# Edge-feature rows of 128 columns, transposed by one DMA per window, and a running maximum kept in PSUM

## Chip, cores and metric

One NeuronCore of a Trainium2 chip runs the whole program. The metric is device time in microseconds (us), the median over runs. The document also uses one execution recorded by the hardware profiler: its page, its waits and its timelines.

## What is computed

A graph of 6,250 nodes and 206,250 directed edges, 16 features a node and an edge, goes through two layers. The second layer is the one that the change touches. Cut to what matters:

```python
h = relu(layernorm(x))                                  # (6250, 16)
w_m = (efeat @ W_msg  + b_msg ).reshape(E, 16, 16)      # per edge
w_a = (efeat @ W_attn + b_attn).reshape(E, 16, 16)
h_src = h[src][:, :, None]
e1, e2 = w_m * h_src, w_a * h_src
seg_max = segment_max(e2, dst)
ex = exp(e2 - seg_max[dst])
ft = segment_sum(e1 * ex / segment_sum(ex, dst)[dst], dst)
out = x + ft.sum(axis=1)
```

The first layer gathers a row of a precomputed table (node times relation weight) for every edge and sums the rows over each destination node.

## The kernel before, in words

**Windows.** Nodes are sorted by degree and laid on 128 partitions, so a partition holds one destination node. A *window* takes up to 48 edges (slots) of each of 128 nodes. A node with more edges goes through more windows, and a maximum and two sums are carried on. The number of slots that a window uses comes from a plan made on the chip. In the second layer they are counted in *halves* of 3 slots (`nh`, 6 to 16 of them) and *blocks* of 6 (`nb`). There are 50 windows; the loop over `pairs` has two of them in its body, `q` = 0 and 1.

**Edge features.** During the first layer, VectorE splits each edge's 16 features into bf16 parts (`split_chunk`), and SyncE writes them out as rows of `KE` = 100 bf16 columns into a DRAM tensor `ef6`, in 50 chunks. In the second layer GpSimd's queue fetches a window's rows by one indirect DMA into `efrow` (`edge_rows`): each partition receives 48 rows end to end. `edge_valid` on VectorE writes the last column of every row, which masks slots past the node's last edge.

**Transposes.** TensorE needs a slot's features along partitions. `transposes(w, t)` transposes eight slots with eight matmuls against an identity into PSUM (`psTb`), and ScalarE copies them to `efT` (`copy_T`), which has two buffers. Six such steps make a window. Those for window k+1 are issued inside window k: two after the weights of the message phase have begun, and one in each of the blocks 0 to 3 of the message phase. `efrow` has one buffer, so GpSimd waits for the last transposes before it fetches the next window's rows.

**Phase 1, scores.** For each half, TensorE makes the attention weights of 3 slots (`weights(0, q, h, ...)`, line 562, into one of two PSUM buffers `psW`), and in between adds the exponentials of the window before (`exp_sums`, line 568). VectorE multiplies the weights by the gathered node features (`times_h`, line 1187) into `score`. After each block it raises a running maximum `macc`, 6 slots wide in SBUF: line 1198 for blocks 0 and 1 together, line 1203 for each later block, line 1206 for an odd last half. Then it folds the 6 slots to one: 3 slots with 3 (helper line 787, 128x768), line 1210 and line 1211 (256 wide), and one more into `mnew` in PSUM (line 787 again), and line 1214 takes the difference to the old maximum.

**Phase 2, messages.** For each block VectorE subtracts the maximum (`from_max`, line 1218), multiplies the message weights by the node features (line 1187 again, into `prod`), and multiplies by the exponentials that ScalarE made (line 717; the product is line 1231). TensorE adds up the products (`prod_sums`, line 573) and closes each block with a small matmul that frees a `prod` buffer (line 620). At a window's end VectorE can go on only when TensorE has added the last products and has made the first weights of the next window.

**Gathers.** GpSimd's queue issues one indirect DMA per slot (line 359), one window ahead, paced by counters that VectorE raises.

Of the kernel before, what the change touches and what calls it, by code (L numbers as in the profile page):

```python
# [6 lines left out]
BF16 = mybir.dt.bfloat16  # L7
I32 = mybir.dt.int32
I16 = mybir.dt.int16
# [8 lines left out]
PN = 125  # L18
# [20 lines left out]
KE = 6 * D + 4  # L39
HI, MID, LO = 0, 3 * D, 5 * D  # L40
# [20 lines left out]
def build(nc, x, src, dst, efeat, etype, relw, loopw, relemb, wmsg, bmsg, wattn, battn, out, scratch):  # L61
    table_d, srcp_d, pairp_d, _, h2_d, first_d, info_d = scratch
    ef6_d = nc.dram_tensor("ef6", ((E + S) * KE,), BF16, kind="Internal").ap()
    ctx = ExitStack()
    with ctx:
# [27 lines left out]
        winhot, winrel = at(o + 2 * WCH, WCH, GC), at(o + 3 * WCH, WCH, GC)  # L93
        lhs = at(21200, 3 * GP, GC).rearrange("p (j n) -> p j n", j=3)
# [4 lines left out]
        ef6 = at(3 * CHR * D, CHR * KE).bitcast(BF16).rearrange("p (q r k) -> p q r k", q=2, k=KE)  # L99
# [7 lines left out]
        stage = sb("stage", [128, RING * BLK * IO + S * KE // 2 + S * GP])  # L107
        prod = stage[0:GP, 0:RING * BLK * IO]
        o2 = RING * BLK * IO
        efrow = stage[0:GP, o2:o2 + S * KE // 2].bitcast(BF16)  # L110
        efs = efrow.rearrange("p (s k) -> p s k", k=KE)
        o2 += S * KE // 2
        efT = stage[0:KE, o2:o2 + S * GP].bitcast(BF16).rearrange("k (q s n) -> k q s n", q=2, n=GP)
        tabgn = stage[127:128, o2:o2 + NW // 2].bitcast(I16)
# [13 lines left out]
        macc = work[0:GP, 0:BLK * IO].rearrange("p (s c) -> p s c", c=IO)  # L128

        def col256(j, n=1):  # L130
            return work[0:GP, BLK * IO + j * IO:BLK * IO + (j + n) * IO]
# [16 lines left out]
        tri = sb("tri", [PN, PN])  # L148
# [5 lines left out]
        nodei = sb("nodei", [PN, C + 1], I32)  # L154
        nodeid = sb("nodeid", [PN, C + 1])
        iotai = sb("iotai", [GP, NV], I32)
        iotaf = sb("iotaf", [GP, NV])
        firsts = sb("firsts", [PN, RPP])
        cnt = sb("cnt", [PN, C + 1])
        rowi = sb("rowi", [PN, C + 1], I32)  # L160
        start0 = sb("start0", [PN, C + 1])
        key = sb("key", [PN, C])
        rank = sb("rank", [PN, C])
        ranki = sb("ranki", [PN, C], I32)
# [28 lines left out]
        mnew = psT[0:GP, 8:10, :].rearrange("p a n -> p (a n)")  # L193
        psTb = psT[:, :, :].rearrange("p a n -> p (a n)").bitcast(BF16).rearrange("p (t s n) -> p t s n", t=3, n=128)
# [9 lines left out]
                 "hg0 hg1 hl0 hl1 h_free efT_ps efT_sb w_ready w_free d_ready c_ready "  # L204
# [30 lines left out]
        def _(sp):  # L235
# [19 lines left out]
            for a in range(2):  # L255
                sp.dma_start(ef6_d[E * KE + a * (S * KE // 2):E * KE + (a + 1) * (S * KE // 2)].rearrange("(a b) -> a b", a=1),
                             padrow[:, 0:S * KE // 4].bitcast(BF16)).then_inc(m["pad_out"], 16)
# [22 lines left out]
            ef6rows = ef6_d[0:E * KE].rearrange("(p c n) -> p c n", p=PN, c=ECH)  # L280
# [17 lines left out]
            for j in range(2):  # L298
                sp.wait_ge(m[f"ef6_out{j}"], 16 * (ECH // 2))

        @block.gpsimd
        def _(pool):
# [91 lines left out]
            def edge_rows(q):  # L395
                pool.indirect_dma_start(out=efrow, out_offset=None, in_=ef6_d.rearrange("(e k) -> e k", k=KE),
                                        in_offset=bass.IndirectOffsetOnAxis(ap=ebst[:, q:q + 1].bitcast(U32), axis=0)).then_inc(m["ef_in"], 16)
# [51 lines left out]
            with pool.Fori(0, pairs) as i:  # L449
                for q in range(2):  # L450
# [31 lines left out]
                    pool.wait_ge(m["efT_ps"], k * (S // 8) + (S // 8))  # L482
# [11 lines left out]
        def _(pe):  # L494
# [58 lines left out]
            def transposes(w, t):  # L553
                pe.wait_ge(m["efT_sb"], w * (S // 8) + (t + 1))
                for j in range(8):
                    last = nc.tensor.transpose(psTb[0:KE, t % 2, j, 0:GP], efs[:, 8 * t + j, :], identb[0:GP, 0:GP])  # L556
                last.then_inc(m["efT_ps"], 1)

            def weights(c0, q, h, at0):
                pe.wait_ge(m["w_free"], at0 + (h + 1))  # L560
                for j in range(HALF):
                    last = nc.tensor.matmul(psW[0:GP, h % 2, j * IO:(j + 1) * IO], efT[:, q, h * HALF + j, 0:GP],  # L562
                                            wst[:, c0:c0 + IO], start=True, stop=True)
# [14 lines left out]
            pe.wait_ge(m["valid_in"], 1)  # L578
            for t in range(S // 8):
                transposes(0, t)  # L580
            with pe.Fori(0, pairs) as i:
                for q in range(2):
# [4 lines left out]
                    pe.wait_ge(m["efT_sb"], k * (S // 8) + (S // 8 + 2))  # L587
# [13 lines left out]
                    pe.wait_ge(m["valid_in"], k + 2)  # L601
                    for t in range(2):
                        transposes(k + 1, t)
                    pe.wait_ge(m["sum_read"], k + 1)
                    nc.tensor.matmul(psS[0:GP, :], ident[0:GP, 0:GP], carry, start=True, stop=False)
                    for b in range(NBW):
# [6 lines left out]
                        if b + 2 < S // 8:  # L613
                            transposes(k + 1, b + 2)
# [17 lines left out]
        def _(act):  # L632
# [90 lines left out]
            for t in range(S // 8):  # L723
                copy_T(0, 0, t)
            act.wait_ge(m["m0_ready"], 1)
            with act.Fori(0, pairs) as i:
                for q in range(2):
# [14 lines left out]
                    for b in range(NBW):  # L742
# [7 lines left out]
                        if b < S // 8:  # L750
                            copy_T(k + 1, 1 - q, b)
# [533 lines left out]
```

## Time and profile before

| | |
|---|---|
| median of 3 runs | 5954.85 us (5950.09 to 5958.16) |
| the profiled execution | 5951.75 us, span 5949.9 us |
| mean granted TensorE clock | 0.935 |
| busy: TensorE matmul / VectorE / ScalarE / GpSimd | 46% / 58% / 23% / 70% |
| second layer, steady part | 3200 to 5900 us of the span |

Busy shares are averages over stages with different limits, so they are read stage by stage. In a timeline, "idle before" stands in brackets with what ended it. A start minus the start before it, on one engine, gives what an instruction costs in its place, and this is often less than its own duration, since neighbours overlap a little.

### The profile page before, as it was taken

To read this page: it belongs to the slowest core of one execution; us is meant where nothing else is said; L and a number is where in the kernel's file an instruction comes from. 1 tells how busy PE (TensorE), PEld (TensorE's weight loads), DVE (VectorE), ACT (ScalarE), POOL (GpSimd) and SP (SyncE) were. 2 spreads that over 40 slices of the span, in tenths; PEclk is the share of its full clock that TensorE was granted. 3 is DMA by queue.
4 is the path that set the end of the run, shared out by engine and by line. 5 is a ranking of instruction groups with operands and counts; after the bars stand their busy time and mean duration, and the time that the engine had idled before them with its cause. 6 is when DMAs were issued, how large, how long until landed. Compare 5 with 4: busy or idle time off the path is not lost.

```text
span 5949.9 us, 57446 instructions
## 1 busy us (share of the span) xinstructions
PE 2723.7 (46%) x13577; PEld 1930.7 (32%) x13578; DVE 3470.4 (58%) x4171; ACT 1369.4 (23%) x1709; POOL 4176.8 (70%) x3713
## 2 busy tenths in 40 slices
PE   2550000000000000000668888788888888878887
PEld 1110000000000000000446666565656565655565
DVE  8601222222222223332688888888888888888886
ACT  2540000000000000010223232333333333333333
POOL 2237777777777777765477878777777777777763
PEclk9999999999999999999978888888889888988998
DMA  4881111111111111110111111111111111111110
GB/s 145 285 264 27 29 22 28 29 30 35 29 29 36 29 36 36 36 34 19 21 22 22 22 24 28 22 22 30 22 22 30 22 30 22 30 22 30 30 30 19
DMA packets 157959, 251.69 MB, mean 42 GB/s; under 512 B 73726, under 2 KB 130563, under 8 KB 145156
## 3 DMA queue, kind: packets, MB, share of 16 engines
q0 software_dynamic: 126192, 100.10, 9.4%
q1 hardware_dynamic: 31711, 151.31, 7.7%
q8 instruction: 9, 0.15, 0.0%
q14 instruction: 15, 0.12, 0.0%
q10 hardware_dynamic: 32, 0.01, 0.0%
HBM read 113.57 MB, written 136.63 MB: 42 GB/s over the span
## 4 chain that ended last, share of the span: by engine, by line
POOL 28%; PE 23%; issue 15%; DVEq 14%; DVE 12%; DMA 5%; POOLq 1%; ACT 1%; SPq 0%; ACTq 0%
POOL gath L359 26%; PE psS L568 10%; PE psS L573 8%; DVEq L1228 7%; DVE stage L1187 4%; DMA table<-arena 4%; PE psW L562 3%; DVE stage L1231 3%; DVEq L1194 2%; DVEq L1187 1%; DVEq L1156 1%; PE psW L516 1%; DVEq L1143 1%; ACT arena L650 1%; DVE arena L1187 1%
## 5 line engine op out<-in xcount | busy, mean ns | idle before, releaser
L359 POOL DMA_INDIRECT gath<-h_dram,hidx x1695 | 2119.4, 1250 | 732.2 <-issue 556.0
L359 POOL DMA_INDIRECT gath<-table,blkidx x1646 | 1639.6, 996 | 508.2 <-issue 505.0
L556 PE MATMUL psT<-identb,stage 128*100 128x128 bf16 x2448 | 226.2, 251 | 2340.2 <-DVEq L1143 2321.9
L573 PE MATMUL psS<-stage,ident 128*128 128x256 f32 x3390 | 930.1, 430 | 169.6 <-DVE stage L1231 169.1
L556 PEld LDWEIGHTS psT<-identb,stage 128*100 128x100 bf16 x2448 | 201.6, 150 | 2380.7 <-DVEq L1143 2279.7
L568 PE MATMUL psS<-arena,ident 128*128 128x256 f32 x3390 | 823.8, 380 | 0.2 <-issue 0.2
L573 PEld LDWEIGHTS psS<-stage,ident 128*128 128x128 f32 x3390 | 705.3, 216 | 322.0 <-DVE stage L1231 212.4
L787 DVE TENSOR_TENSOR work<-gath 128x768 f32<-128x768 f32 x50 | 48.2, 965 | 1284.9 <-DMA gath<-table,blkidx 1284.9
L1187 DVE TENSOR_TENSOR arena<-psW,gath 128x768 f32 (+1 forms) x565 | 523.7, 952 | 438.0 <-PE psW L562 301.5
L562 PE MATMUL psW<-wst,stage 100*128 100x256 bf16 x3390 | 574.5, 290 | 241.6 <-DVE arena L1187 164.9
L717 ACT ACTIVATE arena<-arena 128x1536 f32<-128x1536 f32 (+1 forms) x294 | 421.4, 1433 | 894.4 <-DVE arena L1218 894.4
L568 PEld LDWEIGHTS psS<-arena,ident 128*128 128x128 f32 x3390 | 601.3, 190 | 69.1 <-issue 0.4
L1187 DVE TENSOR_TENSOR stage<-psW,gath 128x768 f32 (+1 forms) x565 | 514.1, 950 | 14.8 <-issue 14.8
L1231 DVE TENSOR_TENSOR stage<-stage,arena (+1 forms) x294 | 499.0, 1697 | 31.4 <-ACT arena L717 5.5
L1218 DVE TENSOR_TENSOR arena<-arena,psT 128x1536 f32 (+2 forms) x294 | 495.3, 1685 | 0.0
L678 ACT ACTIVATE work<-work 128x48 f32<-128x48 f32 x50 | 12.1, 243 | 2065.2 <-DVE work L1041 2065.2
L562 PEld LDWEIGHTS psW<-wst,stage 100*128 100x128 bf16 x3390 | 294.9, 101 | 519.7 <-DVE arena L1187 203.6
L1203 DVE TENSOR_TENSOR work<-work,arena 128x1536 f32<-128x1536 f32 x171 | 300.7, 1758 | 15.8
L712 ACT ACT_TABLE_LOAD x50 | 64.2, 1283 | 1042.1 <-PE psS L576 1042.1
L707 ACT COPY stage<-psT 100x1024 bf16<-100x1024 bf16 x306 | 301.2, 997 | 10.8 <-PE psT L556 10.8
L516 PE MATMUL psW<-stage,work 102*125 102x460 bf16 x400 | 182.4, 609 | 185.7 <-ACT arena L650 154.4
L650 ACT COPY arena<-psW 125x920 f32<-125x920 f32 x200 | 175.4, 927 | 203.8 <-DMA table<-arena 149.6
(227 smaller groups left out, 2395.4 us busy)
## 6 DMA issues: line engine op xcount, KB each, us to landing
table<-arena SPq DMA_DIRECT2D x50, 1610.0 KB
ef<-arena SPq DMA_DIRECT2D x50, 805.7 KB
gath<-h_dram,hidx POOLq DMA_INDIRECT x1695, 2.4
gath<-table,blkidx POOLq DMA_INDIRECT x1646, 2.4
arena<-in_edge_attr SPq DMA_DIRECT2D x50, 257.8 KB
table<-arena SPq DMA_DIRECT2D x50, 186.9 KB
arena<-first_dram POOLq DMA_DIRECT2D x1, 915.5 KB, 12.3
info<-info_dram POOLq DMA_DIRECT2D x2, 432.0 KB, 10.4
```

The source lines that it names most:

```text
L359: pool.indirect_dma_start(out=gath[:, q, s, :], out_offset=None, in_=rows, in_offset=bass.IndirectOffsetOnAxis(ap=idx[:, q, s:s + 1].bitca ...
L556: last = nc.tensor.transpose(psTb[0:KE, t % 2, j, 0:GP], efs[:, 8 * t + j, :], identb[0:GP, 0:GP])
L562: last = nc.tensor.matmul(psW[0:GP, h % 2, j * IO:(j + 1) * IO], efT[:, q, h * HALF + j, 0:GP], wst[:, c0:c0 + IO], start=True, stop=True)
L568: nc.tensor.matmul(psS[0:GP, 0:IO], ident[0:GP, 0:GP], score[:, q, s, :], start=False, stop=False)
L573: nc.tensor.matmul(psS[0:GP, IO:2 * IO], ident[0:GP, 0:GP], prod[:, c0:c0 + IO], start=False, stop=False)
L707: nc.scalar.copy(efT[:, q, 8 * t:8 * t + 8, 0:GP], psTb[0:KE, t % 2, :, 0:GP]).then_inc(m["efT_sb"], 1)
L717: nc.scalar.activation(v, v, ACT.Exp).then_inc(m["exp_done"], 1)
L1187: V.tensor_tensor(dst_ap.rearrange("p s (i o) -> p s i o", o=D), psW[0:GP, s, 0:HALF * IO].rearrange("p (s i o) -> p s i o", i=D, o=D), bc ...
L1203: V.tensor_tensor(macc, macc, score[:, q, ds(b * BLK, BLK), :], ALU.max).then_inc(m["scored"], 1)
L1218: V.tensor_tensor(blk, blk, mnew.unsqueeze(1).to_broadcast([GP, n, IO]), ALU.subtract).then_inc(m["sub_done"], 1)
L1228: V.drain()
L1231: V.tensor_tensor(pr, pr, score[:, q, ds(b * BLK, n), :].rearrange("p s c -> p (s c)"), ALU.mult).then_inc(m["q_ready"], 1)
```

## The change

- Rows of `ef6` have `KP` = 128 columns in place of 100. The 28 new columns are zero. DRAM tensor, chunk writes and the indirect fetch grow in that proportion.
- The 48 TensorE transposes and six ScalarE copies of a window go. SyncE issues one transposing DMA per window, from `efrow` (128 x 6144 bf16) to `efT[:, q]` (128 x 48 x 128). It waits for `valid_in` (the mask column is written) and `efT_free` (the weights of two windows ago have been read).
- TensorE waits at the head of a window for the whole transposed window (`efT_in`), and at its end has a 16-column matmul on zeros that raises `efT_free`. GpSimd waits for `efT_in` before it fetches the next rows.
- `macc` is 3 slots wide and lies in PSUM, in the banks that the transposes used. Each full block takes two 768-wide maxima with a drain between them, in place of one 1536-wide. Blocks 0 and 1 take three such instructions (one after block 0, two after block 1) in place of one of 1536. The final fold is three 256-wide maxima.
- Several small tiles of the first stages move into the arena, and ScalarE waits once for `idx_ready`.

```diff
-            def transposes(w, t):
-                pe.wait_ge(m["efT_sb"], w * (S // 8) + (t + 1))
-                for j in range(8):
-                    last = nc.tensor.transpose(psTb[0:KE, t % 2, j, 0:GP], efs[:, 8 * t + j, :], identb[0:GP, 0:GP])
-                last.then_inc(m["efT_ps"], 1)
-            def copy_T(w, q, t):
-                act.wait_ge(m["efT_ps"], w * (S // 8) + (t + 1))
-                nc.scalar.copy(efT[:, q, 8 * t:8 * t + 8, 0:GP], psTb[0:KE, t % 2, :, 0:GP]).then_inc(m["efT_sb"], 1)
...
+            def transpose_rows(w, q):
+                sp.wait_ge(m["valid_in"], w + 1)
+                sp.sem_inc(m["passed"], 1)
+                sp.wait_ge(m["efT_free"], w + 1)
+                sp.sem_inc(m["passed"], 1)
+                sp.dma_start_transpose(efT[:, q, :, :], efrow).then_inc(m["efT_in"], 16)
...
-                    pool.wait_ge(m["efT_ps"], k * (S // 8) + (S // 8))
+                    pool.wait_ge(m["efT_in"], k * 16 + 16)
                     pool.sem_inc(m["passed"], 1)
                     edge_rows(1 - q)
...
-                    pe.wait_ge(m["efT_sb"], k * (S // 8) + (S // 8 + 2))
+                    pe.wait_ge(m["efT_in"], k * 16 + 16)
...
+                    nc.tensor.matmul(psS[0:GP, IO:IO + D], zero[:, 0:GP], zero[:, 0:D], start=False, stop=False).then_inc(m["efT_free"], 1)
...
-            V.memset(ef6[:, :, :, KE - 1:KE], 0.0)
+            V.memset(ef6[:, :, :, KE - 1:KP], 0.0)
...
+                    def raise_max(b, halves=2):
+                        for s in range(halves):
+                            if s:
+                                V.drain()
+                            last_op = V.tensor_tensor(macc, macc, score[:, q, ds(b * BLK + HALF * s, HALF), :], ALU.max)
+                        return last_op
+
                     scores(0)
+                    V.tensor_tensor(macc, score[:, q, 0:HALF, :], score[:, q, HALF:BLK, :], ALU.max)
                     scores(1)
-                    V.tensor_tensor(macc, score[:, q, 0:BLK, :], score[:, q, BLK:2 * BLK, :], ALU.max).then_inc(m["scored"], 2)
+                    raise_max(1).then_inc(m["scored"], 2)
...
-                        V.tensor_tensor(macc, macc, score[:, q, ds(b * BLK, BLK), :], ALU.max).then_inc(m["scored"], 1)
+                        raise_max(b).then_inc(m["scored"], 1)
...
                     edge_valid(k + 1, 1 - q)
-                    tt(macc[:, 0:HALF, :], macc[:, 0:HALF, :], macc[:, HALF:BLK, :], ALU.max)
+                    V.drain()
                     dve.wait_ge(m["mold_ready"], k + 1)
-                    V.tensor_tensor(macc[:, 0, :], macc[:, 0, :], macc[:, 1, :], ALU.max)
-                    V.tensor_tensor(macc[:, 2, :], macc[:, 2, :], mold, ALU.max)
-                    V.drain()
-                    tt(mnew, macc[:, 0, :], macc[:, 2, :], ALU.max)
+                    tt(ratio, macc[:, 2, :], mold, ALU.max)
+                    tt(ratio, macc[:, 1, :], ratio, ALU.max)
+                    tt(mnew, macc[:, 0, :], ratio, ALU.max)
```

## Rows read from the trace of the kernel before

**Rows 1.** The page, busy time, share of the span and instructions of each engine.
```profile
PE 2723.7 (46%) x13577; PEld 1930.7 (32%) x13578; DVE 3470.4 (58%) x4171; ACT 1369.4 (23%) x1709; POOL 4176.8 (70%) x3713
```

**Rows 2.** Busy time by stretch: first layer, steady second layer; clock, DMA, GB/s last.
```profile
370.00:2708.00 2338.00, 43.12 (x92) 14.70 (x91) 615.84 (x1398) 192.29 (x253) 1690.84 (x1700) 1.00 0.16 39
...
3200.00:5900.00 2700.00, 2212.05 (x11500) 1632.76 (x11500) 2313.28 (x2265) 898.45 (x1130) 2024.88 (x1600) 0.88 0.12 26
```

**Rows 3.** Waits of VectorE, 3200 to 5900 us: total us, times, longest.
```profile
DVE arena L1187 <- PE psW L562: 273.8, 180, 5.3
```

**Rows 4.** Timeline of VectorE in phase 1 of one window: start, us, instruction.
```profile
4546.23 0.96 DVE L1187 TENSOR_TENSOR arena<-psW,gath 128x768 f32<-128x768 f32 x1 [0.67 <-PE psW L562]
...
4552.49 1.76 DVE L1203 TENSOR_TENSOR work<-work,arena 128x1536 f32<-128x1536 f32 x1
4554.17 1.81 DVE L1187 TENSOR_TENSOR arena<-psW,gath 128x768 f32 x2
```

**Rows 5.** Timeline of VectorE, the fold at the end of that phase 1.
```profile
4563.70 0.96 DVE L787 TENSOR_TENSOR work<-work 128x768 f32<-128x768 f32 x1
4564.73 0.43 DVE L1210 TENSOR_TENSOR work<-work 128x256 f32<-128x256 f32 x1
...
4565.56 0.43 DVE L787 TENSOR_TENSOR psT<-work 128x256 f32<-128x256 f32 x1
...
4566.41 1.75 DVE L1218 TENSOR_TENSOR arena<-arena,psT 128x1536 f32<-128x1536 f32 x1
```

**Rows 6.** The page, costliest groups: count, then busy us, mean ns, idle before.
```profile
L556 PE MATMUL psT<-identb,stage 128*100 128x128 bf16 x2448 | 226.2, 251 | 2340.2 <-DVEq L1143 2321.9
...
L1203 DVE TENSOR_TENSOR work<-work,arena 128x1536 f32<-128x1536 f32 x171 | 300.7, 1758 | 15.8
```

**Rows 7.** Groups of VectorE by line over the whole span.
```profile
L1198 DVE TENSOR_TENSOR work<-arena 128x1536 f32<-128x1536 f32 x50 | 88.0, 1760 | 4.6
...
L1206 DVE TENSOR_TENSOR work<-work,arena 128x768 f32<-128x768 f32 x23 | 22.0, 958 | 2.1
```

**Rows 8.** Timeline of TensorE where one window ends and the next begins.
```profile
4541.67 0.28 PE L620 MATMUL psS<-zero 1*128 1x256 bf16 x1
4542.45 0.50 PE L562 MATMUL psW<-wst,stage 100*128 100x256 bf16 x3 [0.50 <-issue]
```

**Rows 9.** Timeline of VectorE, the first product of two other windows.
```profile
4288.23 0.96 DVE L1187 TENSOR_TENSOR arena<-psW,gath 128x768 f32<-128x768 f32 x1 [3.59 <-PE psW L562]
...
4418.89 0.96 DVE L1187 TENSOR_TENSOR arena<-psW,gath 128x768 f32<-128x768 f32 x1 [5.28 <-PE psW L562]
```

**Rows 10.** TensorE by stretch: busy us (count), granted clock, DMA share, GB/s.
```profile
4406.00:4413.00 7.00, 4.14 (x21) 1.00 0.07 5
4413.50:4417.00 3.50, 3.34 (x8) 0.53 0.10 4
```

**Rows 11.** All engines by stretch while edge rows come in; DMA share, GB/s last.
```profile
4544.00:4546.00 2.00, 2.00 (x14) 1.61 (x12) 0.96 (x1) 0.00 (x0) 1.64 (x2) 1.00 1.00 274
4546.00:4548.00 2.00, 2.00 (x13) 1.70 (x12) 1.10 (x2) 0.00 (x0) 1.45 (x2) 1.00 0.85 349
```

**Rows 12.** DMA queues (packets, MB, share of 16 engines) and issues (median us to landing).
```profile
q0 software_dynamic: 126192, 100.10, 9.4%
...
stage<-ef,ebst POOLq DMA_INDIRECT x51, 6.0
```

**Rows 13.** Timelines of VectorE and TensorE in one of the shortest windows.
```profile
5795.14 0.33 DVE L1142 TENSOR_SCALAR stage<-iotaf,erem 128x48 bf16<-128x48 f32 x1
...
5827.29 0.50 PE L562 MATMUL psW<-wst,stage 100*128 100x256 bf16 x3
```

**Rows 14.** Timelines of GpSimd and VectorE early in the second layer.
```profile
2921.37 0.94 POOL L359 DMA_INDIRECT gath<-h_dram,hidx  x1 [9.40 <-DVE work L1198]
2922.61 2.37 POOL L359 DMA_INDIRECT gath<-h_dram,hidx  x1 [0.30 <-issue]
...
2986.88 1.82 DVE L1187 TENSOR_TENSOR arena<-psW,gath 128x768 f32 x2 [14.57 <-DMA gath<-h_dram,hidx]
```

More of the change, by code:

```diff
@@ L39 @@
 KE = 6 * D + 4
+KP = 128
 HI, MID, LO = 0, 3 * D, 5 * D
@@ L93, in build @@
         winhot, winrel = at(o + 2 * WCH, WCH, GC), at(o + 3 * WCH, WCH, GC)
+        tri = at(21600, PN, PN)
+        nodei = at(21725, C + 1, PN, I32)
+        nodeid = at(21776, C + 1, PN)
+        iotai = at(21827, NV, GP, I32)
+        cnt = at(21955, C + 1, PN)
+        rowi = at(22006, C + 1, PN, I32)
+        start0 = at(22057, C + 1, PN)
+        key = at(22108, C, PN)
+        rank = at(22158, C, PN)
+        ranki = at(22208, C, PN, I32)
         lhs = at(21200, 3 * GP, GC).rearrange("p (j n) -> p j n", j=3)
@@ L105, in gtmp @@
             return at(o + NROW + (C + 1) * ROW + i * C * D, GC * D, GP).rearrange("p (c d) -> p c d", d=D)
-        stage = sb("stage", [128, RING * BLK * IO + S * KE // 2 + S * GP])
+        stage = sb("stage", [128, RING * BLK * IO + S * KP // 2 + S * GP])
         prod = stage[0:GP, 0:RING * BLK * IO]
         o2 = RING * BLK * IO
[L110 to L114, printed above, removed]
+        efrow = stage[0:GP, o2:o2 + S * KP // 2].bitcast(BF16)
+        efs = efrow.rearrange("p (s k) -> p s k", k=KP)
+        o2 += S * KP // 2
+        efT = stage[0:KP, o2:o2 + S * GP].bitcast(BF16).rearrange("k (q s n) -> k q s n", q=2, n=GP)
         tabtmp = stage[0:1, 4608:4608 + NW // 2].bitcast(I16)
@@ L299, in _ @@
                 sp.wait_ge(m[f"ef6_out{j}"], 16 * (ECH // 2))
+            def transpose_rows(w, q):
[4 more added lines that the diff above has]
+                sp.dma_start_transpose(efT[:, q, :, :], efrow).then_inc(m["efT_in"], 16)
+            sp.wait_ge(m["win_ready"], 16)
+            pairs = sp.value_load(npair[0:1, 0:1], min_val=(GC + 1) // 2, max_val=NW // 2 - 2)
+            with sp.Fori(0, pairs) as i:
+                for q in range(2):
+                    transpose_rows(2 * i + q, q)
+            transpose_rows(2 * pairs, 0)
+            sp.wait_ge(m["efT_in"], pairs * 32 + 16)
+            sp.sem_inc(m["passed"], 1)
         @block.gpsimd
@@ L561, in weights @@
                 for j in range(HALF):
-                    last = nc.tensor.matmul(psW[0:GP, h % 2, j * IO:(j + 1) * IO], efT[:, q, h * HALF + j, 0:GP],
+                    last = nc.tensor.matmul(psW[0:GP, h % 2, j * IO:(j + 1) * IO], efT[0:KE, q, h * HALF + j, 0:GP],
                                             wst[:, c0:c0 + IO], start=True, stop=True)
@@ L722, in _ @@
             act.reg_mov(cumb, 0)
-            for t in range(S // 8):
-                copy_T(0, 0, t)
             act.wait_ge(m["m0_ready"], 1)
+            act.wait_ge(m["idx_ready"], 2)
             with act.Fori(0, pairs) as i:
@@ L761, in _ @@
             V = nc.vector
-            for name, n in (("tbl_sb", 2), ("l0_math", 2), ("h_free", 2), ("efT_sb", 2), ("w_free", 2), ("q_free", RING)):
+            for name, n in (("tbl_sb", 2), ("l0_math", 2), ("h_free", 2), ("efT_free", 2), ("w_free", 2), ("q_free", RING)):
                 dve.sem_inc(m[name], n)
```

41 lines of the change are left out of this document (11 added, 30 removed).

## The prediction

> **What bounds the kernel now.** I read the page's busy shares first [rows 1]. GpSimd leads with 70% over the span, which is no answer, since the stages differ. So I read the busy times by stretch next [rows 2]. In the first layer (370 to 2708 us) GpSimd's queue is busy 1691 of 2338 us, issuing gathers one after the other, and everything else waits for them. In the second layer, 3200 to 5900 us, VectorE is busy 2313 of 2700 us and TensorE 2212. The change is worked out there. VectorE's waits then say when it isn't VectorE that counts [rows 3]: 273.8 us of waiting for the weights, in 180 places over 45 windows, so four in each. A window's timeline shows which four. One is the handover between windows, 3 to 5 us. The other three are 0.67 us each, in the second to fourth half of phase 1 [rows 4], where TensorE gives a half every 0.67 + 0.96 = 1.63 us and VectorE needs 0.96. From the fifth half on, VectorE waits for TensorE no more until the window ends. So a window's length is VectorE's instruction stream, plus the handover, plus three short waits.
>
> **The change part by part.** All sums are made against the profiled execution, 5951.75 us, 3 us under the median of the runs.
>
> *Transposes and copies.* 2448 TensorE transposes, 226 us of busy time [rows 6], and ScalarE's six copies a window go. I cost this at nothing. They lie in phase 2 and just before it, where VectorE has no gap and TensorE waits for VectorE's products; ScalarE is busy 898 of 2700 us [rows 2]. The cover is VectorE's stream. Without it a window would gain up to 226/51 = 4.4 us. No transpose stands in the handover or between the first halves, the places where VectorE waits.
>
> *Running maximum.* A full block's maximum now costs 4554.17 - 4552.49 = 1.68 us from start to start [rows 4]. The new one is a 768-wide instruction with a drain behind it, then another. With SBUF operands the first costs 4564.73 - 4563.70 = 1.03 [rows 5], and a second that the next instruction overlaps costs about 0.87 (0.96 less the 0.08 by which 1.76 exceeds 1.68). Together 1.90, or 0.22 more; I take 0.23, since writing to PSUM in place of SBUF adds at most 0.01 to a 256-wide one, 0.43 each [rows 5]. No row reads and writes PSUM in one VectorE instruction. Reading it costs nothing visible: 0.96 from PSUM [rows 4], 0.958 from SBUF [rows 7]. Bounds for the pair are 1.86 and two full 1.03, so 0.18 to 0.38 more. It applies to 171 later blocks [rows 6] and to block 1 in 50 windows [rows 7], all behind the last short wait: 221 x 0.23 = +51 us (40 to 84). The maximum after block 0 takes about 1.0 us and falls between the second and third half, where 0.67 is waiting. The third half starts some 0.35 late, and the fourth waits for TensorE anyway, so 0 (up to 17 for 50 windows). The 23 odd halves stay at one 768-wide instruction, 0.
>
> The Trainium skill, "VectorE: DVE Perf Modes", section on the TRN2 errata, gives a VectorE instruction a fixed part of 58 cycles with an SBUF source and 120 with a PSUM source at 0.96 GHz. By it each PSUM-source instruction is an estimated 0.065 us dearer, and some 615 of them (442 in pairs, 23 odd, 150 in folds) would add 40 us, for a total near 6007. The rows do not agree, with 0.96 against 0.958 us at the same width, and the sum goes by them.
>
> *Fold.* Before, from the 768-wide fold to the subtraction, 4566.41 - 4563.70 = 2.71 us [rows 5]. After: a drain on an empty pipe (about 0.05), three dependent 256-wide maxima at 0.51 each (0.43 plus 0.08 of drain) and the difference at 0.34, together 1.92. Saved 0.79, times 50 is -40 us (-36 to -43).
>
> *Handover.* TensorE gets one small matmul between the last products and the next weights. Its wide sister takes 0.28 us and is followed by 0.50 us in which the engine waits for its own instructions [rows 8]. Below 0 nothing is possible, above 0.28; I take 0.1, so +5 us (0 to 14).
>
> *The transposing DMA.* It moves 128 x 6144 x 2 B = 1.57 MB. No row shows one. The nearest from below is the row fetch, which runs at about 311 GB/s [rows 11] (its 1.23 MB land 6.0 us after issue [rows 12]), giving 5.0 us plus about 2 for issue and landing: 7. From above: every 256 B piece as a packet of its own, at the gathers' mean of 9.4% x 16 x 5949.9 / 126192 = 71 ns of an engine [rows 12], so 6144 x 71 ns / 16 = 27 us. I take 15, nearer the fetch than the gathers. Its cover is phase 2. In one of the shortest windows (47.5 us long), mask written at 5795.5, first weights at 5827.3: 31.8 us [rows 13]. The mean window is 2700/45 = 60 us, with some 40 in the same proportion. So 0 at either bound. If it were late, TensorE stands at the head of the window, and behind it the weights for VectorE. GpSimd's new wait stands behind a whole window of gathers. Behind it are the row fetch, the output scatter and the next gathers, and it is the looser of the two. SyncE has nothing else queued.
>
> *Wider rows.* A chunk write grows by 28%, under 1 us at 311 GB/s; it lies beside GpSimd's stream, 0. The row fetch goes from 6.0 to about 7.5 us and has the 15 us and more of phase 1, 0. The larger memset happens once, 0 to 2 us. ScalarE's wait for `idx_ready` is over before it has work.
>
> *GpSimd relieved.* A gather takes 2.37 us, not 0.94, where it meets the 1536-wide maximum with its two SBUF inputs [rows 14]. That ends for the maxima. It counts only where VectorE waits for gathers, which after the first window is 14.57 us [rows 14] and once more a few. -4 us (-18 to 0).
>
> Sum: +51 - 40 + 5 - 4 = +12. 5951.75 + 12 = 5964; against the median 5955 + 12 = 5967. I give 5966. What a measurement of this kernel can tell from no change is about 0.2%, 12 us, so this lies at its edge.
>
> **The rivals.**
>
> *TensorE's clock at the handover (the faster side).* VectorE waits 5.28 us there in some windows and 3.59 in others that end alike [rows 9], two of 48. In the former the clock fell to half after a thinly used stretch (4.14 of 7 us busy at full clock, then 0.53) [rows 10]. About 20 of 48 windows have the fall. Which ones depends on how gaps fall together, and window lengths change. If all lost it, 14 even ones x 1.65 and 9 others at about 0.8 give -31: 5966 - 31 = 5935. Against it: the last two blocks never had many transposes, and their gaps stay. It decides once eight or more windows lose the fall and GpSimd's relief gives its 18. The reverse, all windows falling, is +30: 5996. Stretches with weights and no transposes ran at full clock [rows 10], so I see no fall in mid-phase.
>
> *PSUM maxima at their dear bound.* 84 in place of 51, the third half's 17 and the handover's 14: 5966 + 33 + 17 + 9 = 6025. For it: nobody shows a PSUM-to-PSUM instruction. Against it: each side alone costs nothing.
>
> *The transposing DMA outlasts phase 2.* The engines may cut the write into pieces smaller than 256 B, since a transposed row is scattered over partitions; this is also the case in which the change does not do what it says. From 31.8 us on, short windows lengthen. At 50 us, against some 40 of cover on average, it is 10 x 49 = +490: 6450. If pieces were 64 B, four times 27 is 108, and then (108 - 40) x 49 = +3330: 9300. For it: nothing here bounds the pieces. Against it: the row fetch ran at 274 to 349 GB/s.
>
> **How the numbers follow.** The sum as it stands has 0.62, with a range of its own from 5943 to 6000. Clock and relief together 0.13, dear maxima or a worse clock 0.12, late DMA 0.13. The predicted time is the first's. The range 5938 to 6025 leaves out the late DMA and a little of the fast side, 0.18 in all. Faster by over 0.2% (under 5943): 0.04 of the first and 0.12 of the second, 0.16. Within: 0.38 of the first and 0.02 of others, 0.40. Slower: 0.20 + 0.12 + 0.12, 0.44.
>
> **What would show it.** Pairs of 768-wide maxima at 1.90 us from start to start; a fold of 1.9 us; no wait of TensorE for `efT` at a window's head, and the DMA landing within 27 us; handover waits still spread from about 3 to 5.3 us; phase 2 without new waits. The prediction is wrong if VectorE has gaps before its first product that end with the transposing DMA, or if a PSUM maximum takes more than 1.03 us, or if the handover waits move together to one side.

## The result, and the profile after

The changed kernel takes 5975.89 us (median of 8 runs, 5972.98 to 5982.7), the kernel before 5955.94 us in the same comparison: ratio 1.0035, 95% interval 1.0024 to 1.0046, so 14 to 27 us slower. The forecast was 5966 us, with a range of 5938 to 6025. On the third of the four chips that the experiments used, one execution of the kernel before took 7991 us, the ten others 6266 to 6302; it enters no ratio. The profiled execution has a span of 5974.9 us and a mean granted clock of 0.925.

The page's busy times, against [rows 1], and the busy times by stretch, against [rows 2]:

```profile
PE 2587.0 (43%) x11179; PEld 1765.6 (30%) x11180; DVE 3512.5 (59%) x4392; ACT 1092.2 (18%) x1403; POOL 3938.9 (66%) x3713
```
```profile
370.00:2708.00 2338.00, 48.53 (x103) 16.46 (x103) 604.87 (x1375) 196.44 (x251) 1697.64 (x1703) 1.00 0.18 45
3200.00:5900.00 2700.00, 2093.34 (x9395) 1489.32 (x9394) 2341.33 (x2442) 658.13 (x862) 1824.22 (x1608) 0.86 0.26 57
```

In the steady stretch TensorE is relieved of 119 us and ScalarE of 240. Neither shows in the time, for VectorE sets the pace there, and its busy time rises by 28. VectorE in phase 1 of one window, against [rows 4], and in its fold, against [rows 5]:

```profile
4502.26 0.96 DVE L1184 TENSOR_TENSOR arena<-psW,gath 128x768 f32<-128x768 f32 x1 [3.60 <-PE psW L573]
4503.89 0.96 DVE L1184 TENSOR_TENSOR arena<-psW,gath 128x768 f32<-128x768 f32 x1 [0.67 <-PE psW L573]
4504.94 0.97 DVE L1201 TENSOR_TENSOR psT<-arena 128x768 f32<-128x768 f32 x1
4505.82 0.95 DVE L1184 TENSOR_TENSOR arena<-psW,gath 128x768 f32<-128x768 f32 x1
4507.14 0.96 DVE L1184 TENSOR_TENSOR arena<-psW,gath 128x768 f32<-128x768 f32 x1 [0.38 <-PE psW L573]
...
4512.01 2.01 DVE L1197 TENSOR_TENSOR psT<-psT,arena 128x768 f32<-128x768 f32 x2
4513.93 1.81 DVE L1184 TENSOR_TENSOR arena<-psW,gath 128x768 f32 x2
...
4523.54 0.34 DVE L1139 TENSOR_SCALAR stage<-iotaf,erem 128x48 bf16<-128x48 f32 x1
4524.05 0.93 DVE L784 TENSOR_TENSOR work<-psT,work 128x256 f32<-128x256 f32 x2 [0.17 <-issue]
4525.05 0.43 DVE L784 TENSOR_TENSOR psT<-psT,work 128x256 f32<-128x256 f32 x1
...
4525.89 1.75 DVE L1222 TENSOR_TENSOR arena<-arena,psT 128x1536 f32<-128x1536 f32 x1
```

Read starts, not durations. A pair of maxima takes 4513.93 - 4512.01 = 1.92 us where one instruction took 1.68: 0.24 more, 221 times, +53 us. The maximum after block 0 (line 1201) fills what was a wait for TensorE, and of the three short waits one and a half are left: the fourth half starts 4507.14 - 4502.26 = 4.88 us after the first, just as before (4547.86 - 4542.98). From the mask (line 1139) to the subtraction (line 1222) it is 4525.89 - 4523.54 = 2.35 us. Before, the mask started here:

```profile
4563.25 0.33 DVE L1142 TENSOR_SCALAR stage<-iotaf,erem 128x48 bf16<-128x48 f32 x1
```

To the subtraction at 4566.41 that is 3.16 us, so 0.81 less now, 50 times, -40 us.

The groups of VectorE by line: all 465 in-place PSUM maxima (2 x 221 and 23 odd halves), mean 967 ns, against 958 from SBUF [rows 7].

```profile
L1197 DVE TENSOR_TENSOR psT<-psT,arena 128x768 f32<-128x768 f32 x465 | 449.5, 967 | 38.9
```

The handover on TensorE, against [rows 8], and the waits of VectorE, 3200 to 5900 us, against [rows 3]:

```profile
4501.50 0.28 PE L623 MATMUL psS<-zero 1*128 1x256 bf16 x1
4501.62 0.17 PE L625 MATMUL psS<-zero 1*128 1x16 bf16 x1
4501.72 0.50 PE L573 MATMUL psW<-wst,stage 100*128 100x256 bf16 x3
```
```profile
DVE arena L1184 <- PE psW L573: 225.3, 133, 5.3
```

Three waits a window are left of four, and VectorE's waits for gathers or the transposing DMA do not appear in the stretch at all. That DMA on SyncE's queue, the DMA share by stretch around it (share and GB/s last), and the queues, against [rows 12]:

```profile
4524.08 7.33 SPq L307 DMA_TRANSPOSE stage<-stage  x1
```
```profile
4524.00:4526.00 2.00, 0.00 (x0) 0.00 (x0) 1.73 (x5) 1.69 (x2) 0.00 (x0) 0.90 0.39 76
4526.00:4528.00 2.00, 0.00 (x0) 0.00 (x0) 2.00 (x3) 0.74 (x2) 0.94 (x1) 0.50 1.16 217
4528.00:4530.00 2.00, 1.34 (x2) 0.50 (x2) 1.46 (x4) 1.16 (x1) 1.69 (x2) 0.50 1.14 210
4530.00:4532.00 2.00, 0.73 (x1) 0.00 (x0) 1.27 (x3) 0.00 (x0) 1.39 (x3) 0.50 1.15 210
4532.00:4534.00 2.00, 1.64 (x6) 0.56 (x6) 1.90 (x2) 0.00 (x0) 1.63 (x2) 0.50 0.61 96
```
```profile
q1 hardware_dynamic: 346687, 243.09, 15.3%
q0 software_dynamic: 126192, 117.65, 10.0%
```

The window's rows are transposed between some 4525 and 4533 us; TensorE wants them 30 us later. Queue q1 had 31,711 packets before, so the 51 transposing DMAs are 6,176 packets each. At 1.57 MB that is 255 B a packet on average, which would fit 6,144 pieces of 256 B and 32 small ones; no row shows the split.

**The window as a whole.** The timelines between 3200 us and the last handover of the stretch hold 44 whole windows in each kernel. Mean us of one, and VectorE's idle time in it by place (from the waits in brackets, summed; the finish is the short arithmetic that closes the window before):

| kernel | window | handover | phase 1 | fold and finish | phase 2 | rest: VectorE's stream |
|---|---|---|---|---|---|---|
| before | 60.58 | 4.09 | 2.01 | 0.71 | 0.41 | 53.37 |
| after | 60.81 | 3.99 | 1.05 | 0.91 | 0.41 | 54.45 |

That is +0.23 us a window, +10 for the 44. From the first handover to the last, with the early windows that wait for gathers, the two profiles differ by less: 2970.5 against 2962.7 us, +7.8. Behind the last handover the changed kernel takes 75.9 us against 74.3, +1.6. The other 15.6 us of the 25 between these two executions stand before the first handover (2928.47 against 2912.90), 11.2 of them in the stage in which the window tables and the relation table are built.

### The profile page after: what moved, and what is told of

It reads as the page before. It is cut to its first block, busy times and chain, and to the rows that moved or that the text cites. A ratio compares the mean times of both kernels' runs of the same rounds, so it can differ in the third digit from the quotient of the medians.

```text
span 5974.9 us, 52495 instructions
## 1 busy us (share of the span) xinstructions
PE 2587.0 (43%) x11179; PEld 1765.6 (30%) x11180; DVE 3512.5 (59%) x4392; ACT 1092.2 (18%) x1403; POOL 3938.9 (66%) x3713
## 4 chain that ended last, share of the span: by engine, by line
POOL 28%; PE 20%; issue 15%; DVEq 15%; DVE 13%; DMA 5%; POOLq 1%; ACT 1%; SPq 0%; ACTq 0%
POOL gath L376 26%; PE psS L584 8%; PE psS L579 8%; DVEq L1232 6%; DMA table<-arena 4%; DVE stage L1184 4%; DVEq L1191 3%; PE psW L573 3%; DVE stage L1235 3%; DVE psT L1197 2%; DVEq L1184 1%; DVEq L1143 1%; PE psW L533 1%; ACT arena L654 1%; DVE work L784 1%
## 5 line engine op out<-in xcount | busy, mean ns | idle before, releaser
L376 POOL DMA_INDIRECT gath<-h_dram,hidx x1695 | 1915.9, 1130 | 992.8 <-issue 549.3
L584 PE MATMUL psS<-stage,ident 128*128 128x256 f32 x3390 | 982.4, 449 | 256.3 <-DVE stage L1235 255.9
L584 PEld LDWEIGHTS psS<-stage,ident 128*128 128x128 f32 x3390 | 739.9, 226 | 448.0 <-DVE stage L1235 324.8
L1197 DVE TENSOR_TENSOR psT<-psT,arena 128x768 f32<-128x768 f32 x465 | 449.5, 967 | 38.9
L610 PE MATMUL psS<-efraw,ident 128*128 128x512 f32 x100 | 103.6, 1140 | 277.6 <-DVEq L1153 277.6
L533 PEld LDWEIGHTS psW<-stage,work 102*125 (+1 forms) x400 | 59.6, 206 | 317.2 <-ACT arena L654 242.1
L347 POOL DMA_INDIRECT info_dram<-arena x50 | 59.0, 1180 | 118.3 <-DVEq L910 94.1
```

Source lines behind the costliest of these rows:

```text
L376: pool.indirect_dma_start(out=gath[:, q, s, :], out_offset=None, in_=rows, in_offset=bass.IndirectOffsetOnAxis(ap=idx[:, q, s:s + 1].bitca ...
L533: last = nc.tensor.matmul(psW[0:PN, u % 2, 512 * a:512 * a + PIECE], hT6[:, ds(2 * t + j, 1), 0:PN].rearrange("k a n -> k (a n)"), relW6[: ...
L584: nc.tensor.matmul(psS[0:GP, IO:2 * IO], ident[0:GP, 0:GP], prod[:, c0:c0 + IO], start=False, stop=False)
L1197: last_op = V.tensor_tensor(macc, macc, score[:, q, ds(b * BLK + HALF * s, HALF), :], ALU.max)
```

## The experiments

The first four were timed on one chip, the next four on another, with the kernel before beside each. Ratios are to that kernel.

**1. The kernel before, again** (a comment changed).

> The kernel before, once more, for a second profile of it. In the first pair of profiles the changed kernel is 25 us longer, and 11.2 us of that stand before its first layer begins (first product of the first layer at 526.7 in place of 515.5 us) and 15.6 us before the second handover of the second layer (2928.5 in place of 2912.9). Theory A, the extra in the table stage is chance of single executions: this profile puts the first product anywhere from 510 to 530 us. Theory B, it belongs to the changed kernel: this profile puts it within 2 us of 515.5.

Measured: 5964.77 us, ratio 1.0000 (0.9990 to 1.0011). The last copy of the table stage, at 436.27 us in the profile of before and 447.51 in that of after, came here at 459.15, and the first handover at 2937.22. The first product of the first layer stands at 538.4 us, later than either theory had it. A later beginning of this size comes without the change. In the four profiles with the early stages of before (number 8 is one) the first handover stands at 2912.90, 2920.20, 2923.27 and 2937.22 us, in five of the changed kernel and its variants at 2921.04 to 2928.47, so no shift there stands out from that scatter. The 44 windows have 60.64 us.

**2. Placement alone**, **3. wide rows alone**, **4. the changed kernel with the maximum as before.** Number 2 is the kernel before with the larger DRAM tensor, number 3 the kernel before with 128 columns and the moved tiles, TensorE still transposing. Number 4 keeps the transposing DMA; it holds a table of window codes of 3,072 entries in place of 4,608, and this input uses some 50. Number 4 also brings back the 1536-wide maxima that read two SBUF inputs.

```diff
# 2
-    ef6_d = nc.dram_tensor("ef6", ((E + S) * KE,), BF16, kind="Internal").ap()
+    ef6_d = nc.dram_tensor("ef6", ((E + S) * 128,), BF16, kind="Internal").ap()[0:(E + S) * KE]
# 3
+KP = 128
-    ... KE (ef6_d, ef6, efrow, efs, ef6rows, edge_rows)
+    ... KP
# 4, against the changed kernel
-        macc = psT[0:GP, 0:2 * HALF, :]...
+        macc = work[0:GP, 6 * IO:6 * IO + BLK * IO]...
-                    raise_max(1).then_inc(m["scored"], 2)
+                    V.tensor_tensor(macc, score[:, q, 0:BLK, :], score[:, q, BLK:2 * BLK, :], ALU.max).then_inc(m["scored"], 2)
...
```

> The kernel before with only the DRAM tensor ef6 made as large as the changed kernel's, 128 columns a row; its rows stay at 100 columns and end to end, the rest is never touched. No instruction differs. Theory A (chance) and theory C (the wider rows' own traffic in the first layer): no change, ratio 1.000 within 0.001. Theory B (the place of tensors in DRAM sets the rate of the table writes): first product of the first layer at about 526 us and 8 to 12 us longer.

> One part of the change alone: rows of 128 columns in DRAM, in the chunk writes, in the fetch and in efrow, and the small tiles moved into the arena. The 48 TensorE transposes, the six copies and the running maximum in SBUF stay. If my sum holds (wider rows cost nothing) and the table stage is chance: 0 to +2 us. If the wider rows or their place cost what the profiles show ahead of the second layer: +8 to +15 us, with the first layer's end 4 us and the table's end up to 11 us later.

> The changed kernel with the running maximum undone: six slots wide in SBUF, one 1536-wide maximum a block and the old fold. The transposing DMA stays. For room the table of window codes is cut from 4608 to 3072 entries, of which this input uses some 50. The sum says that the new maximum costs 221 x 0.24 = +53 us and its fold saves 50 x 0.81 = 40 us, so undoing both takes 13 us off the changed kernel: ratio to the kernel before about 1.0013, near 5963 us. Rival: the extra lies in the transposing DMA or in the stages before it; then this stays at 5972 to 5976 us. Under the clock rival the handover waits would differ as a group, by 15 us or more.

Measured: 5961.91 us, 0.9996 (0.9987 to 1.0006); 5959.96 us, 0.9997 (0.9988 to 1.0006); 5968.97 us, 1.0007 (0.9997 to 1.0016). By these intervals neither place nor width costs more than 4 us, the row fetch of 28% more bytes included. With the maximum back in SBUF, 0.0007 is left, of 0.0035 in the first comparison and 0.0028 in number 5. So the maximum and its fold are the main part, 13 to 17 us of 17 to 20, where the two terms make 13. Number 4 and the changed kernel were not timed on the same chip, so this is a difference of two ratios. The transposing DMA with all that it took away is worth 0.0007, its interval reaching to nothing.

Number 4 also tells what relieves GpSimd. Its steady stretch, all engines, GpSimd's queue the fifth:

```profile
3200.00:5900.00 2700.00, 2092.61 (x9411) 1499.82 (x9410) 2308.07 (x2252) 656.92 (x861) 2023.43 (x1606) 0.85 0.26 57
```

The queue is busy 2023 us, as before the change (2025), against 1824 with the maximum in PSUM. It is the new maximum that gives GpSimd 200 us back, and not the transposing DMA.

**5. The changed kernel, again.**

> The changed kernel, measured again beside the one before. If the first comparison (ratio 1.0035) tells what the change costs, this one gives 1.002 to 1.005. If it came from chance beginnings of the window-table stage (11 us later in the profiled execution of the changed kernel, and up to 12 us later in another execution of the kernel before itself), it gives under 1.002, and the profile's steady part, from the second handover between windows to the last, still shows about 8 us more than the 2962 to 2965 us of the kernel before.

Measured: 5978.57 us, 1.0028 (1.0018 to 1.0038). The first theory holds. The same 44 windows in all profiles of this kind, mean us of one:

| kernel | window | handover | window without handover and phase 2's idle time |
|---|---|---|---|
| before | 60.58 | 4.09 | 56.08 |
| 1, before again | 60.64 | 4.14 | 56.09 |
| 2, placement alone | 60.64 | 4.14 | 56.09 |
| 3, wide rows alone | 60.80 | 4.28 | 56.11 |
| 4, changed, maximum as before | 60.76 | 4.22 | 56.13 |
| changed | 60.81 | 3.99 | 56.41 |
| 5, changed again | 60.90 | 4.08 | 56.41 |
| 7, changed, four small matmuls | 60.84 | 4.06 | 56.38 |

The last column repeats to some hundredths and moves with the maximum alone: 0.28 us between number 4 and the changed kernel, 14 us for 50 windows. The handover scatters by up to 0.2 us between profiles of kernels with equal medians (numbers 2 and 3 against each other: 0.14; before against 3: 0.19), 9 us for 48 handovers, so the sum of one profile does not settle 10 us.

**6. Four transposing DMAs in a row per window.**

```diff
-                sp.dma_start_transpose(efT[:, q, :, :], efrow).then_inc(m["efT_in"], 16)
+                for n in range(4):
+                    sp.dma_start_transpose(efT[:, q, :, :], efrow).then_inc(m["efT_in"], 16)
+                    if n < 3:
+                        sp.wait_ge(m["efT_in"], w * 64 + 16 * (n + 1))
```

> The changed kernel with the transposing DMA of each window given four times, each after the one before has landed. One pass is read off the DMA engines' busy stretch as 9 to 10 us, so four take 37 to 40 us, against a cover of 31.8 us in the shortest window and of some 40 us in most. Theory that the single pass is wholly hidden with 22 us or more to spare: 5 to 30 us slower than the changed kernel, all of it in waits of TensorE at its first weights of a window, and nothing on VectorE's waits for the gathers. Rival that the pass already costs something by itself, because it takes DMA engines and the SBUF from the gathers: three more passes cost three times that at the gathers too, VectorE's waits for gathered rows grow from 132 us, and the kernel is 40 us or more slower.

Measured: 6127.38 us, 1.0287 (1.0271 to 1.0303), 149 us more than number 5. Its stretches of 1 us (DMA share and GB/s last) show one pass from edge to edge, and the start of the next:

```profile
4524.00:4525.00 1.00, 0.00 (x0) 0.00 (x0) 0.85 (x3) 0.99 (x2) 0.00 (x0) 0.79 0.04 7
4525.00:4526.00 1.00, 0.00 (x0) 0.00 (x0) 0.93 (x3) 0.69 (x2) 0.00 (x0) 0.50 1.12 215
...
4532.00:4533.00 1.00, 0.96 (x6) 0.34 (x4) 0.90 (x2) 0.00 (x0) 0.69 (x2) 0.50 0.68 125
4533.00:4534.00 1.00, 0.40 (x2) 0.00 (x0) 1.00 (x1) 0.00 (x0) 0.60 (x1) 0.50 0.08 8
...
4535.00:4536.00 1.00, 1.00 (x4) 0.73 (x4) 1.00 (x1) 0.00 (x0) 0.77 (x1) 0.50 0.90 175
```

A pass keeps the DMA engines busy 7.7 us, the next starts 10.1 us after its start, and the fourth ends at 4562.6, 39 us after the mask. TensorE's waits in the stretch 3200 to 5900 us:

```profile
PE psW L577 <- DMA stage<-stage: 85.3, 24, 8.2
```

So at some 40 us the third rival's mechanism is there: a window takes 64.12 us, VectorE's handover wait 6.58 and its phase 1 wait 1.75, and its stream is unchanged (54.48). The gathers were not held up: VectorE's waits for them are 124.2 us (132.2 with one pass). The size was far above what I expected (5 to 30), since I had set the cover at 40 us for most windows, and it is about what four passes take, so about every second window pays. A late window also costs more than TensorE's wait: behind one of 3.18 us, from 5628 to 5631 us, the granted clock was 0.58, and VectorE's second wait there was 1.94 us in place of 0.67.

**7. Four small matmuls at the handover in place of one.**

```diff
+                    for _ in range(3):
+                        nc.tensor.matmul(psS[0:GP, IO:IO + D], zero[:, 0:GP], zero[:, 0:D], start=False, stop=False)
```

> The changed kernel with four of the small 1-row, 16-column matmuls at the end of each window in place of one. In the trace the one takes 0.17 us and moves the next matmul by 0.10 us. Theory that it stands on the path (VectorE waits there for the first products' weights): three more cost 3 x 0.10 x 50 = 15 us, ratio 1.0025 to the changed kernel. Rival that they overlap, or that the handover's length is set by the granted clock alone: within 5 us of the changed kernel.

Measured: 5972.44 us, 1.0026 (1.0015 to 1.0037), so not slower than number 5; my own theory fell. The distance from the closing matmul of the last block to the next weights, the most frequent value of 44 or 45 handovers, is 0.21 us before, 0.22 after and 0.29 here. A small matmul takes 0.01 to 0.03 us there, for it begins before its neighbour has ended. The mean distance, with the handovers in which TensorE stands still on its own, is 0.54 us before, 0.57 to 0.59 in two profiles of the changed kernel and 0.60 here.

**8. Early weights, on the kernel before.** The first two groups of weights of the next window are made ahead of the last block's product sums, so that VectorE finds them.

```diff
-                        with pe.If(nb > b):
+                        with pe.If(nb > b + 1):
                             pe.wait_ge(m["q_ready"], tb + (b + 1))
...
+                    for h in range(2):
+                        weights(0, 1 - q, h, tn * 4)
+                    pe.wait_ge(m["q_ready"], tn)
+                    for b in range(MINB - 1, NBW):
+                        with pe.If(nb > b):
+                            with pe.If(nb < b + 2):
+                                prod_sums(2 * b)
...
```

> The kernel before, with the next window's first two groups of four weight products made ahead of the last block's product sums, so that VectorE finds them at the handover. My reading of the handover is that VectorE stands still there for 3.6 us on average (183 us over the 45 handovers listed past 3200 us, 1 us of it for the end of its own pipe) while TensorE finishes the product sums and then makes the weights. Theory: nearly all of that goes, 45 to 50 times 3 us = 130 to 170 us, 5790 to 5830 us. Rival: the two groups need psum space and the granted clock that the last product sums need as well, or the finish of the window then waits for sum_done, and VectorE loses at the maximum or at the finish what it gains at the handover: 0 to 60 us gained.

Measured: 5981.34 us, 1.0047 (1.0033 to 1.0061). Both theories had expected a gain. The handover's wait fell from 4.1 to 1.31 us a window, and phase 1's rose from 2.01 to 4.84. TensorE and VectorE there:

```profile
4851.92 0.28 PE L576 MATMUL psS<-zero 1*128 1x256 bf16 x1
4855.51 0.50 PE L562 MATMUL psW<-wst,stage 100*128 100x256 bf16 x3 [3.31 <-issue]
```
```profile
4850.40 1.82 DVE L1206 TENSOR_TENSOR arena<-psW,gath 128x768 f32<-128x768 f32 x2 [2.32 <-PE psW L562]
4856.05 0.96 DVE L1206 TENSOR_TENSOR arena<-psW,gath 128x768 f32<-128x768 f32 x1 [3.83 <-PE psW L562]
```

Behind the last product sums TensorE stands 3.31 us and waits for no other engine. The granted clock was 1.00 before and during this stretch, 0.64 in the 2.5 us behind it and 0.73 in the 3 us after that, so the weights that follow are late twice over. My edit finds the last block by a row of nested tests there; in the kernel before, the tests for the last blocks come while TensorE waits for VectorE. That the tests make the gap is my reading; number 10 moves them and has no gap.

**9. Two transposing DMAs**, as number 6. **10. Early weights with the test inside the loop over blocks**, where TensorE has time. **11. The same on the changed kernel. 12. Number 10 again.**

```diff
                         with pe.If(nb > b):
+                            if b + 1 >= MINB:
+                                with pe.If(nb < b + 2):
+                                    for h in range(2):
+                                        weights(0, 1 - q, h, tn * 4)
                             pe.wait_ge(m["q_ready"], tb + (b + 1))
```

> The changed kernel with the transposing DMA of each window given twice. In the run with four passes one pass keeps the DMA engines busy 7.7 us at some 207 GB/s, the next begins 10.1 us after it, and four end 40.1 us after the mask of the last column; TensorE waited for them in about half of the windows. Two end after about 20 us, the next window's first weights are due after 31.8 us in the shortest window. Theory that a pass costs nothing until it lands too late: within 6 us of the changed kernel, ratio to the kernel before 1.002 to 1.004, and no wait of TensorE for the DMA. Rival that the traffic itself costs time, by holding up gathers or SBUF accesses of VectorE: a third of what three more passes cost (149 us), so some 50 us more, ratio 1.011.

> The kernel before, with the next window's first two groups of weight products made ahead of the last block's product sums, now tested for inside the loop over blocks, so that the tests run while TensorE waits for VectorE anyway. In the first form TensorE stood 3.3 us in its own sequencer behind the last product sums (in the window looked at) and VectorE lost there, at the third half, what it gained at the first. Theory that those tests were all that ate the gain: the third half comes 2 us or more earlier in each window, 80 to 130 us gained, 5830 to 5880 us. Rival that the sequencer's time belongs to the start of a window and is only no longer hidden: the wait before the third half stays near 3 us and the time within 20 us of the kernel before.

> The same edit on the changed kernel. The weights of the next window now need the transposing DMA 4 to 6 us earlier, against 22 us to spare in the shortest window, so that costs nothing. Theory: it gains as much here as on the kernel before, and the difference of the two stays 10 to 20 us. Rival: the maximum's cost of 0.24 us per block pair or the fold's gain changes its worth where the handover no longer sets VectorE's start, and the two come out equal within 6 us.

> The kernel before with early weights and the test inside the loop over blocks, measured again, because the last comparison came from a chip on which the kernel before itself took 6283 us and VectorE had long waits that no semaphore explains, in every stage. In the window read there TensorE goes from the last product sums to the third group of weights with no gap, and VectorE waits 2.38 + 1.18 + about 0.67 us over the first four halves where the kernel before waits 4.08 + 3 x 0.67 = 6.09 us on average. On a chip on which the kernel before takes 5950 to 5970 us the theory gives 2 to 3 us per window, 100 to 150 us in all, ratio 0.975 to 0.984. Rival: the ratio of the last comparison, 0.994, is what the edit gives on any chip. If the slow chip comes again, the ratio is 0.992 to 0.996.

Measured: 9 to 11 ran on a third chip, 12 on a fourth. There the kernel before took 6283 and 6284 us.

| | us | ratio |
|---|---|---|
| 9 transposing twice | 6489.26 | 1.0321 (1.0297 to 1.0345) |
| 10 early weights | 6248.57 | 0.9938 (0.9918 to 0.9958) |
| 11 early weights, changed kernel | 6451.66 | 1.0265 (1.0242 to 1.0288) |
| 12 as 10 | 6261.37 | 0.9968 (0.9956 to 0.9980) |

These chips differ before the second layer begins. VectorE's waits in the first layer, 600 to 2600 us, in number 2 and then in number 10:

```profile
DVE work L787 <- DMA gath<-table,blkidx: 1178.1, 45, 41.3
DVE bstf L998 <- issue: 85.9, 45, 2.0
```
```profile
DVE bstf L1007 <- issue: 320.5, 39, 11.7
DVE valid L1042 <- issue: 281.2, 40, 11.2
```

All waits of VectorE there that nothing in the profile releases add up to 182 us (longest 2.0) on the first chips and 1384 us (longest 11.7) here. So VectorE stands still up to 12 us at a time with nothing in the profile to release it. In the second layer part of its waits have a releaser that the profile names only as "remote": 80 us in number 10 and 274 in number 11 (3200 to 6100 us), none in the profiles of the first chips. The times of 9 and 11 can't be read as the cost of a second pass or of early weights alone. One thing can be read from the trace of number 9: from 2950 us on TensorE never waits there for the transposing DMA, as its first theory had it, so two passes a window are still hidden. Set beside each other, 11 and 10 carry the same edit, on the same chip: 6451.66 / 6248.57 = 1.033. Per window (46 of them): 67.67 against 63.07 us, with 3.39 against 0.81 us of VectorE's idle time in fold and finish, 7.24 against 6.12 in phase 1, and 55.3 against 54.2 of stream. There the change seems to cost ten times what it costs on the first chips, mostly in waits; number 11 had been expected to keep the difference at 10 to 20 us. Number 10, repeated as number 12, gains 35 and 23 us over the kernel before (0.9968 is a little short of the 0.992 to 0.996 expected for a slow chip); the changed kernel itself was not timed on these chips. With the tests moved TensorE goes on without a gap:

```profile
5061.04 0.28 PE L629 MATMUL psS<-zero 1*128 1x256 bf16 x1
5061.25 0.50 PE L562 MATMUL psW<-wst,stage 100*128 100x256 bf16 x3
```

Number 10 had been expected to gain 80 to 130 us. Whether it gains that, or the 100 to 150 of number 12, on a chip of the first kind is open, since neither met one.

## Why the prediction came out as it did

The mechanism was right: VectorE's maxima cost what was reckoned, the fold saved what was reckoned, and the rest is small. The total is 10 us short of the median, inside its range, and that gap is only in part explained.

- *What bounds the kernel.* Right: with TensorE and ScalarE relieved and the maximum left as it was, the time does not move measurably (number 4, 1.0007), and VectorE's stream and handover set the window.
- *Transposes and copies, 0.* Right: a block of phase 2 still takes 5.25 us from start to start, and VectorE's idle time in phase 2 is 0.41 us a window in both.
- *Running maximum, +51.* 1.92 where I had 1.90 to 1.91, so +53. The dear bound (84) is out: an instruction that reads and writes PSUM takes 0.967 us, 0.009 more than from SBUF to SBUF. The dearer PSUM source of the Trainium skill ("VectorE: DVE Perf Modes", the TRN2 errata) isn't seen: its figures make an estimated 0.065 more, and the total isn't the 6007 that they gave. The maximum after block 0 was free, as worked out: the fourth half still waits 0.38.
- *Fold, -40.* -40.
- *Handover, +5.* Mis-sized: 0.01 us in the frequent case, +0.5 us in all, and +2 by the means of all handovers (number 7). The 0.50 us of the engine's own waiting in [rows 8] was taken as typical; 28 of 45 handovers in that profile have none of it.
- *Transposing DMA, 15 us, hidden.* It takes some 9 to 10 us from issue to landing, hidden with 22 us to spare in the shortest window. The pieces are about 256 B, as in my upper bound, but one costs an engine about 23 ns (8.9 us of DMA share x 16 / 6144, other traffic included), not 71. The Trainium skill ("DMA: Bandwidth & Descriptors", latency and other measured facts) gives 261 GB/s for a transposing DMA with a non-contiguous middle dimension; number 6 has 204, 1.57 MB in 7.7 us.
- *GpSimd relieved, -4.* VectorE's waits for gathers in the second layer go from 136.5 to 132.2 us. They are 133.8 to 135.1 in numbers 1 to 3 and 132.8 in number 4, so no more than 1 to 4 us is the new maximum's, though it gives GpSimd 200.
- *Clock at the handover.* It reshuffled: in some windows the wait went from 5.28 to 3.60, in others the other way, 4.09 to 3.99 us on average, which is within the scatter of the table in number 5. As a rival it had its mechanism but no direction.
- *Not in the sum.* The finish: VectorE's idle time there is 0.2 us a window longer, of which the fold's 0.17 is counted already. The tail, +1.6, which stands in number 3 too (75.7 us), so it comes with the wide rows or the moved tiles and not with the maximum.

The terms make 53 - 40 + 0.5 - 4 = +9.5, and 1.6 for the tail, +11. The pair of profiles gives +7.8 from the first handover to the last and the same 1.6, +9.4, with 5 us of that pair's handovers on the changed kernel's side; without them it would be +14. The timed difference is 14 to 27 us in the first comparison, 11 to 23 in the second, with medians of 20 and 19. So 6 to 10 us of it lie outside what I can place, and I leave them open. That the sum came within 10 us of the median is no luck of two errors: its two large terms were measured at 53 and 40. The smaller ones, +5 and -4, were each set high, and nearly cancel.

## What to carry to other kernels

Ask what an engine's relief is worth from the engine that sets the pace: 119 us of TensorE time, 240 us of ScalarE time and 200 us of GpSimd's bought next to nothing, while 0.24 us more for a pair of VectorE instructions, 221 times, outweighed the 40 us that the fold saved. Splitting one wide instruction into two narrower ones with a drain between cost 1.92 us here in place of 1.68, and where the space that it frees isn't needed it is better left as it was. Before moving work ahead of a handover, look at what the sequencer does there: with the tests behind the last product sums TensorE stood 3.3 us, with the tests under a wait it did not.

## What was unexpected of the hardware

- A transposing DMA from SBUF to SBUF of 1.57 MB made 6,176 packets and kept the DMA engines busy 7.7 us, at 204 GB/s; the next, issued when it had landed, started 10.1 us after the first.
- A running maximum that reads PSUM and SBUF left GpSimd's queue 1824 us busy in the steady stretch, against 2023 to 2025 with a maximum that reads SBUF twice.
- A 16-column matmul behind a 256-column one delayed its follower by 0.01 us in the most frequent case, though its row says 0.17.
- Two of the four chips of the experiments ran the same kernel 5.4% slower (6283 against 5959 us), with waits of up to 12 us in which no engine, DMA or semaphore of the profile is the cause. What makes them, and why the changed kernel seems to suffer more from them (1.033), is open: the changed kernel itself was not timed there.
